# Another order for TensorE and GpSimd, and another opening, in a Mamba block with its feed-forward layer

## The reference

```
xz = x @ in_proj.T;  x_, z = split(xz)                 # 512 channels each
u  = silu(causal_conv4(x_) + conv_b)
dt_lo, B, C = split(u @ x_proj.T)                      # 64, 16, 16
delta = softplus(dt_lo @ dt_proj.T + dt_b);  A = -exp(A_log)
h_t = exp(delta_t * A) * h_(t-1) + (delta_t * u_t) * B_t   # 512 channels x 16 states
y_t = sum_n h_t[:, n] * C_t[n] + u_t * D
x1  = layernorm(x + (y * silu(z)) @ out_proj.T)
g   = silu(x1 @ w1.T * s1) * (x1 @ w2.T * s2)           # 1024
out = layernorm(x1 + ffn3(gelu(gelu(g @ h1.T * sh1) @ h2.T * sh2)))
```

## Time and profile before

| | us |
|---|---|
| median of three runs | 3078.45 |
| profiled execution | 3078.75 |
| its span | 3077.0 |
| VectorE busy in the span | 2304.9 |
| GpSimd busy | 1703.3 |
| TensorE busy | 2754.1 |

### The profile page before, as it was taken

How to read it: one execution, slowest core, us unless ns; L and a number is a source line. 1 busy time by engine, 2 the same in 40 slices (tenths; PEclk the granted TensorE clock), 3 DMA queues, 4 the chain that set the end, 5 groups by cost and what they waited for, 6 DMA issues and landing times. The chain is left out here.

```text
span 3077.0 us, 40971 instructions
## 1 busy us (share of the span) xinstructions
PE 2754.1 (90%) x11540; PEld 1625.5 (53%) x11540; DVE 2304.9 (75%) x2650; ACT 2038.6 (66%) x3600; POOL 1703.3 (55%) x839
## 2 busy tenths in 40 slices
PE   5788988998898898888898886889999999999997
PEld 1243343343343343343343332678888888888886
DVE  5999999999999999999999999344444444444442
ACT  3778878777877877877877877555555455555442
POOL 3799898898988888988988988300000000000000
PEclk8799999899999999989989987999999999999999
DMA  7466566466476465475475466543222222222210
GB/s 256 105 178 168 135 175 170 122 188 164 124 192 157 129 195 149 135 195 143 139 198 140 141 189 195 198 147 95 69 75 89 68 82 84 80 68 89 75 42 15
DMA packets 239645, 412.04 MB, mean 134 GB/s; under 512 B 23264, under 2 KB 63456, under 8 KB 239456
## 3 DMA queue, kind: packets, MB, share of 16 engines
q1 hardware_dynamic: 175680, 297.67, 35.5%
q10 hardware_dynamic: 63776, 112.22, 11.2%
HBM read 285.55 MB, written 124.26 MB: 133 GB/s over the span
## 5 line engine op out<-in xcount | busy, mean ns | idle before, releaser
L1283 DVE TENSOR_TENSOR_SCAN h<-bank,state,db 128x512 f32<-128x512 f32 x1024 | 1246.0, 1263 | 69.9 <-POOL db L1154 48.7
L1143 POOL TENSOR_TENSOR hc<-h,c_rows 128x1024 f32<-128x1024 f32 x512 | 1200.8, 2374 | 170.7 <-PE bank L660 134.5
L918 ACT ACTIVATE bank<-d_bc,a_neg 128x512 f32<-128x512 f32 x1024 | 693.6, 685 | 204.0 <-DVE h L1283 173.7
L1624 ACT ACTIVATE hring<-s_bank,sc 128x512 f32<-128x512 f32 x248 | 170.4, 687 | 488.6 <-PE s_bank L1557 488.2
L1557 PE MATMUL s_bank<-mid,h_r 128*128 128x512 f32 x2048 | 468.7, 390 | 4.6 <-DVEq L1651 4.6
L1267 DVE TENSOR_TENSOR db<-bank,du_bc 128x2048 f32<-128x2048 f32 x192 | 434.4, 2262 | 6.7 <-issue 6.7
L1557 PEld LDWEIGHTS s_bank<-mid,h_r 128*128 128x128 f32 x2048 | 385.5, 188 | 85.5 <-ACTq L1595 5.0
L732 PE MATMUL bank<-x_t,w 128*128 128x512 f32 x1088 | 372.3, 469 | 39.2 <-ACT ab L995 39.1
L633 PE MATMUL bank<-bc,w_spread 64*128 64x512 f32 x272 | 145.7, 547 | 201.6 <-DVE db L1267 199.9
L660 PE MATMUL bank<-hc,fold_w 128*32 128x512 f32 x2048 | 308.4, 678 | 5.5 <-DVE uz L1307 5.3
L732 PEld LDWEIGHTS bank<-x_t,w 128*128 128x128 f32 x1088 | 207.8, 204 | 190.9 <-issue 101.7
(11 more groups left out here) (147 smaller groups left out, 3740.5 us busy)
## 6 DMA issues: line engine op xcount, KB each, us to landing
ab<-ab ACTq DMA_DIRECT2D x272, 256.0 KB, 3.5
du_bc<-du_rows SPq DMA_DIRECT2D x256, 256.0 KB, 4.8
d_bc<-d_rows SPq DMA_DIRECT2D x256, 256.0 KB, 7.9
s_abr<-ab SPq DMA_DIRECT2D x120, 512.0 KB, 3.9
w<-w ACTq DMA_DIRECT2D x136, 256.0 KB, 3.1
d_rows<-sp_r SPq DMA_DIRECT2D x64, 256.0 KB, 2.6
du_rows<-sp_w SPq DMA_DIRECT2D x64, 256.0 KB, 2.2
x<-res SPq DMA_DIRECT2D x17, 512.0 KB, 8.8
```

The lines of the kernel that those rows point to most:

```text
L918: act.activation(decays[DECAY_BANK[g]][:], d_bc[c % 2][:, j, :], ACT.Exp, scale=a_neg[:, g:g + 1]).then_inc(decay, 1)
L1143: pool.tensor_tensor(hc[:, k % HCSTEPS, at:at + HG], h[:, H_SLOT[k], at:at + HG], c_rows[:, q, :].unsqueeze(1).broadcast_to([P, HG, NT]), ...
L1283: dve.tensor_tensor_scan(h[:, H_SLOT[k], j, :], decays[DECAY_BANK[g]][:], db[:, k % DBSTEPS, j, :], state[:, g:g + 1], ALU.mult, ALU.add). ...
L1624: act.activation(hring[c % RING][:], p_h[m % HBANKS][:], ACT.Gelu, scale=sc[:, 2 + layer, m:m + 1]).then_inc(gelu, 1)
```

## The change

Four things are done.

1. GpSimd: at a slot with n % 4 == 0 the product with B stands first, then both halves of the product with C.
2. TensorE: `FOLD_AFTER` goes from 10 to 9, so that a fold stands at n % 4 == 1 ahead of the spread. `Z_SLOTS` are spread over slots 24 to 37, and in `AB_PLACES` slot 38 goes and 26 comes; some counts that are waited for change with them. The gate's slot stays where it was.
3. The opening: w_in gets a semaphore of its own and xT is loaded right behind it. TensorE makes its first products with these two alone. ScalarE copies them out, and only then takes the exponential of A_log.
4. The four reads of w12 go from slot 40 to 62.

```diff
-Z_SLOTS = range(26, 26 + KI * KM)
+Z_SLOTS = (24, 25, 27, 29, 31, 33, 35, 37)
-FOLD_AFTER = 10
-GATE_AFTER = GC - JC + FOLD_AFTER + 1
+FOLD_AFTER = 9
+GATE_AFTER = GC - JC + FOLD_AFTER + 2
-AB_PLACES = ((23, 0), (25, 0), (28, 2), (30, 2), (32, 2), (34, 2), (36, 2), (38, 1), (40, 1), (41, 0), (44, 2), (46, 2),
+AB_PLACES = ((23, 0), (25, 0), (26, 2), (28, 2), (30, 2), (32, 2), (34, 2), (36, 2), (40, 1), (41, 0), (44, 2), (46, 2),
-W12_FIRST = 40
+W12_FIRST = 62
...
+            sp.dma_start(w_in[:], in_wT.rearrange("(k p) e -> p k e", p=P)).then_inc(w_in_in, 16)
+            load_xT(OPENING)
             for dst, src in (
-                (w_in[:], in_wT.rearrange("(k p) e -> p k e", p=P)),
...
         @block.tensor
         def _(pe):
-            pe.wait_ge(weights_in, 16 * WEIGHTS)
-            pe.wait_ge(consts, 2)
+            pe.wait_ge(w_in_in, 16)
...
-                    pe.wait_ge(ab_sb, ab_done(tile_before(t), (7, 15, 16)[c - 1]))
+                    pe.wait_ge(ab_sb, ab_done(tile_before(t), (8, 15, 16)[c - 1]))
...
-                    elif e in (7, 9):
-                        pe.wait_ge(z_sb, nxt.count(KI, 3 if e == 7 else 4))
+                    elif e in (8, 9):
+                        pe.wait_ge(z_sb, nxt.count(KI, e - 5))
...
             for i in range(X_SLOTS[0], X_SLOTS[-1] + 1):
                 early(OPENING, i)
+            pe.wait_ge(weights_in, 16 * WEIGHTS)
+            pe.wait_ge(consts, 1)
...
         @block.scalar
         def _(act):
-            act.wait_ge(weights_in, 16 * WEIGHTS)
             act.preload_act_table_set(EXP_LN)
-            act.activation(a_neg[:], a_neg[:], ACT.Exp).then_inc(a_exp, 1)
-            act.wait_ge(consts, 2)
...
             for i in range(X_SLOTS[0], X_SLOTS[-1] + 2):
                 early(OPENING, i)
+            act.wait_ge(weights_in, 16 * WEIGHTS)
+            act.activation(a_neg[:], a_neg[:], ACT.Exp).then_inc(a_exp, 1)
+            act.wait_ge(consts, 2)
...
                     if n % JC == 0:
-                        done, at = at_group(t, n - JC)
-                        if exists(done):
-                            times_c(done, at // JC, range(1))
                         now, g = at_group(t, n + JC)
                         if exists(now) and g // JC % QN == QV:
                             times_b(now, g // JC)
-                        if exists(done):
-                            times_c(done, at // JC, range(1, TURNS))
+                        now, g = at_group(t, n - JC)
+                        if exists(now):
+                            times_c(now, g // JC)
```

More of the change, by code:

```diff
@@ L293, in mamba_stage @@
         p_mm, p_dt, p_b, p_y, decays = bank[0:2], bank[2], bank[3], bank[4], bank[5:8]
-        weights_in = sem("weights_in")
+        w_in_in, weights_in = sem("w_in_in"), sem("weights_in")
         zeroed = sem("zeroed")
@@ L391, in mamba_stage @@
         block = ctx.enter_context(nc.Block())
-        WEIGHTS = 12
+        WEIGHTS = 11
         def w12_piece(i):
@@ L401, in _, with load_xT @@
         def _(sp):
+            def load_xT(t):
+                sp.dma_start(xT_sb[:], xT[t.b, :, t.tt * NT:(t.tt + 1) * NT]
+                             .rearrange("(k p) t -> p k t", p=P)).then_inc(xT_in, 16)
+            sp.dma_start(w_in[:], in_wT.rearrange("(k p) e -> p k e", p=P)).then_inc(w_in_in, 16)
+            load_xT(OPENING)
             for dst, src in (
-                (w_in[:], in_wT.rearrange("(k p) e -> p k e", p=P)),
                 (w_xp[:], xp_wT.rearrange("(k p) e -> p k e", p=P)),
@@ L416, in _ @@
                 sp.dma_start(dst, src).then_inc(weights_in, 16)
-            def load_xT(t):
-                sp.dma_start(xT_sb[:], xT[t.b, :, t.tt * NT:(t.tt + 1) * NT]
-                             .rearrange("(k p) t -> p k t", p=P)).then_inc(xT_in, 16)
             def copies(t, c):
@@ L460, in store_x1 @@
                 sp.dma_start(at.rearrange("s p c -> p s c"), res[:]).then_inc(x1_out, 16)
-            load_xT(OPENING)
             for piece, src in enumerate(w[k * P:(k + 1) * P, :] for w in (w1T, w2T) for k in range(KM)):
@@ L1131, in _, with times_c @@
             pool.sem_inc(db_pool, POOL0)
-            def times_c(t, k, turns):
+            def times_c(t, k):
                 q = k % QN
-                for turn in turns:
-                    at = HG * turn
-                    if turn == 0:
-                        if k < QN:
-                            pool.wait_ge(rows_sb, t.count(ROWS, q + 2 if q else 1))
-                        pool.wait_ge(folded, t.count(NK, k - HCSTEPS + 1 + FOLDED0))
+                if k < QN:
+                    pool.wait_ge(rows_sb, t.count(ROWS, q + 2 if q else 1))
+                pool.wait_ge(folded, t.count(NK, k - HCSTEPS + 1 + FOLDED0))
+                for at in range(0, JC, HG):
                     pool.wait_ge(scanned, t.count(NG, JC * k + at + HG + SCANNED0))
```

## The result

The changed kernel takes 3054.43 us (median of 4 runs, 3052.72 to 3056.65), the kernel before 3079.65 (4 runs, 3075.27 to 3082.86): a ratio of 0.9919, 95% interval 0.9902 to 0.9937. It is faster, by 25 us (0.8%) where the prediction had 69, and its time lies above the range of 2996 to 3044. The profiled execution is the longest of the four, 3056.65 us, with a span of 3054.8 us.

A forecast was written before the change was run, and what follows sets the result against it. VectorE, 95% busy in the selective-scan stage, was taken to set the pace. Terms -55 -10 +5 -9.4 +0.5 = -69 us took 3078.75 to 3010 us; 8-in-10 range 2996 to 3044, chance of the forecast 0.62.

The forecast's parts named there:

- GpSimd, -55: GpSimd's product with B ahead of both halves with C: VectorE's 59.4 us of waits for it go, less 4 us.
- TensorE's order, -10: Fold at slot 4k+9 ahead of the spread: last xd product ends earlier, low rows' 12.0 us of waits shrink by 10.
- +5 for new waits: New VectorE waits on TensorE or ScalarE once VectorE is quicker: 5 us lost, upper bound 30 us.
- The opening, -9.4: Before the first scan: subtraction 4.3 us earlier, w12 loads out of the way 5.1 us; first decay at 71.3.
- the prediction's two readings of this place: w12 loads beside d_bc: queues take turns on full engines, moving them gains 5.1 us; undisturbed queues, opening gives only 4.3.
- (a): Rival: GpSimd becomes the bound, more than half of VectorE's wait for B returns, no low-rows gain; 3044 us, chance 0.18.
- (d): Rival: B's start set by something other than its queue place, TensorE's gain lost on the added fold; 3078 us, chance 0.05.
- (c): Rival: TensorE's spread, behind a fold waiting for hc, comes too late for VectorE's db step; slower, 3108 us, chance 0.07.
- Wait for B under 8 us: Sign in the profile after: VectorE's scan waits under 8 us in all for GpSimd's product with B.
- First decay near 71: Sign for the opening: the first decay, at 80.69 us before, comes near 71 us.
- Low rows under 3 us: Sign for TensorE's earlier fold: VectorE's low rows, which waited 12.0 us, wait under 3 us.
- The side remark on the z products: TensorE in the opening: 14 passes from 52.4 us, despite a slow clock, end near 62, ahead of the transfers.

## Why the prediction was wrong

**GpSimd, -55.** The wait for B went as forecast, and B starts 0.3 us behind step K-1 at the place that answers to the earlier trace rows. The step that failed is this: the first half with C ends 4.6 us later, "the second half no later than now", and "So nothing downstream moves". It counted GpSimd's work and not its idle time. At the place of step 15 above, the first half ends 7 us later than in the old order (755.2 for 748.2) and the second 2.3 us later (757.5 for 755.2). In the kernel before, GpSimd stood 128.3 us waiting for folds, so at the earlier trace rows step K-1 was scanned by the time GpSimd was free. The same change takes this wait away. GpSimd is then early, and a B at the head of its queue leaves it idle until step K-1 ends: 134.7 us in about 60.7 blocks (1750 us by 115.3 per tile), 2.2 us each. The prediction had seen this wait ("it now has to wait for step K-1 in that time") and gave it 1.5 us per block of room, but did not ask who wants what stands behind it.

Two things did, by the runs. The scan of step 15 wants the first half with C, since its h buffer is reused after two steps; the prediction did not look at the reuse of h at all. Measured: 26.1 us directly, and 42 of 45 us where block 3 alone has B first. And TensorE wants the pair for the fold, which the same change moved one slot earlier: 58.0 us of waits, and 21.5 us of time for the fold's slot where the buffer's wait is out of the way. By which instructions these waits reach VectorE is not shown. Late x products may be one way: with the buffer moved their copies wait 51.9 us with B first and 21.6 without; but in the changed kernel it is 34.5 against 32.3. And 32.1 us of waits for C cost next to nothing where block 3 alone has B first and the buffer is moved.

**TensorE's order, -10, and +5 for new waits.** The earlier fold was taken for the low rows' gain alone and as help for GpSimd. By itself it was worth 51.9 us: it alone removes the wait for B, all but 1.8 us. The prediction had the two facts side by side (128.3 us of waits for folds, 59.4 for B) and gave the 59.4 to the place of B in the queue. The rows that could have told were the earlier trace rows: half a product with C delays B by 2.36 us there, but the wait for the fold ahead of it by 1.43, and VectorE's wait was 0.65; taking away either would do. The sum counted the gain once, which was right; that the two cures, once together, get in each other's way was not seen. The low rows fell by 3.5 us in the whole change and by 8 (to 3.6) with the old GpSimd order, so the 10 was close for the part by itself. New waits of decays and softplus came to 19 us in the changed kernel and 13 without B first, above the +5 taken and within the 30 set as the upper bound.

**The opening, -9.4.** Measured 7.0 at the first scan and 8.9 by the time of that part alone. Two sizes were off, both to the same side. The subtraction starts at 55.03 us, not 53.8, since VectorE's checks end 1.2 us later: GpSimd's first cast, for which they wait, starts at 20.73 us instead of 19.55, when the first piece of h1 has landed, and SyncE issues these pieces from 11.79 us instead of 10.05. (In the other kernels with this opening the subtraction starts between 54.1 and 55.0.) And the way from there to the first decay became 4.0 us shorter (22.6 to 18.6 us), not 5.1. The 5.1 us were 1.05 MB divided by the 207 GB/s of a full window, as if that rate were fixed, but with the reads in it the same share of the engines moved 255 GB/s. Putting the reads back cost 2.4 us, between the prediction's two readings of this place, 5.1 us and nothing. That is not quite the old state: in the kernel before the reads were issued 2.6 us ahead of d_bc (63.85 and 66.42), in the test 0.4 us behind it (63.59 and 63.21), and the store of w12, which the prediction put at nothing, comes at 50 us instead of 58. Which of the two the other 1.6 us belong to, no run separates.

**Sum.** By the runs: TensorE's order -59.5, opening -8.9, B first +41.5 on top of them: -27, and 25 were measured; of the 2 us between, 1.5 are what the first two lack when put together. The kernel without B first takes 3012.93 us, close to the 3010 forecast for the one with it. That is luck: the forecast had 55 us from B first and 10 from TensorE's order.

**The rivals.** The time lies between (a), 3044, and (d), 3078, but neither is what happened. (a) had waits for B return; none did, and GpSimd's share is 90%. (c) is the nearest in kind: a queue on TensorE held up by a fold that waits for its hc, decided by the lateness of the products with C. But it placed the damage at the spread and the db step, which the earlier trace rows allow 13.6 us, and the trace has no wait of VectorE's db step for a spread. What VectorE's list has instead is the scan's wait for C, and more waits for decays and low rows than without B first (22.2 for 18.1 us, 8.5 for 3.6).

**The signs that were named.** Wait for B under 8 us: yes, none. First decay near 71: 73.67. Low rows under 3 us: 8.5. A tile near 112 us: 115.3 (13 tiles, low rows at 256.81 to 1755.18), for 116.3 before. TensorE's share near 91%: 88% (1534.0 of 1750). The last three said that VectorE was not running freely. The side remark on the z products held: they end at 62.1 us, where it had 62.

The quickest kernels are those with the old GpSimd order and the rest of the change, 3011 to 3014 us (also with the buffer moved, or with B first in block 0 or in block 2 alone); they cannot be told apart.

## What to carry over

When an engine waits for a product, look first at what the producer itself waited for before making it; here an earlier fold gave 52 us where a new order of the producer gave 19. An instruction that waits for an event, put ahead of work that could be done meanwhile, delays everything behind it. That cost nothing in blocks 0 and 2, and 25 and 45 us in blocks 1 and 3, so it is not the engine's idle time that tells the price. List who consumes the delayed work and when, with every buffer's reuse distance, special cases at the wrap first, and look where the engine itself has the least room to catch up. Two cures for one wait are to be timed apart before they are put together.

## What was not expected of the hardware

Four reads of together 1 MB on ScalarE's queue, issued 0.4 us behind the d_bc row's loads on SyncE's, delayed the first decay by 2.4 us (75.85 against 73.45), although the engines are full in that stretch (share 1.06 and 1.07 from 68 to 72 us); 1.05 MB at 207 GB/s would be 5.1 us. A full share is thus not a fixed rate: it was 207 GB/s with the broadcasts alone and 255 GB/s with the reads among them.

TensorE's first products after its 7.62 us of standing still took 5.30 us for 8 passes, and the next 8, after 0.75 us, took 3.70. Starting 8.7 us earlier did not make the first 8 slower than in the earlier trace rows (5.23) here. But they took 5.10 to 6.77 us in the fourteen kernels with this opening and 5.11 to 6.08 in the four with the old one, so this duration varies from one execution to the next. The profile has the granted clock at 1.00 in the stretch of 5.30 us, in that of 6.77, and in that of 5.23, in which the prediction took half of the passes to be slow; so it doesn't show why.
